# GpSimd makes the relative dst rows of a double tile ahead of its edge-list gathers, not behind them

## The reference, cut to what matters

```python
def reference(x, src, dst, edge_attr_64, W1, b1, W2, b2):      # x 6250x64, edge_attr 206250x64, dst sorted
    h = jnp.maximum(_layernorm(x, axis=-1), 0.0)
    msg = h[src] + edge_attr_64
    agg = jax.ops.segment_sum(msg, dst, num_segments=6250)
    return x + (jax.nn.relu(agg @ W1 + b1) @ W2 + b2)
```

## Time and profile before

| | |
|---|---|
| Time, median of 3 runs | 562.6 us (560.68 to 565.33) |
| Profiled execution | 561.41 us, its span 559.8 us |
| TensorE (PE) busy | 486.8 us, 87% of the span |
| VectorE (DVE) busy | 428.1 us, 76% |
| ScalarE (ACT) busy | 355.1 us, 63% |
| GpSimd (POOL) busy | 268.7 us, 48% |
| Mean DMA rate | 132 GB/s |

### The profile page before, as it was taken

One profiled execution on the slowest core, in us unless ns is written; L12 is line 12 of the kernel. 1 busy time (PEld: TensorE's weight loads), 2 busy tenths in 40 slices (PEclk: granted clock), 3 DMA queues, 4 the chain that ended last, 5 costly groups with the idle time before them and its releaser, 6 DMA issues.

```text
span 559.8 us, 27476 instructions
## 1 busy us (share of the span) xinstructions
PE 486.8 (87%) x12541; PEld 427.6 (76%) x12541; DVE 428.1 (76%) x456; ACT 355.1 (63%) x503; POOL 268.7 (48%) x249
## 2 busy tenths in 40 slices
PE   1014999999999999999999999999999999998996
PEld 1013788777888888888888888888888888887895
DVE  4999879667887797777787787777788779766941
ACT  3747667665766767656666666666676676575721
POOL 4483774484375366336357347417437535416200
PEclk9999999998999999989999999999999999899999
DMA  9575167453453543633634635435546354354300
GB/s 201 162 216 165 24 200 193 127 167 105 112 176 102 154 141 100 188 102 97 189 105 117 174 101 150 140 99 151 141 110 180 100 154 138 97 152 123 94 7 9
DMA packets 139623, 73.62 MB, mean 132 GB/s; under 512 B 23644, under 2 KB 137550, under 8 KB 139382
## 3 DMA queue, kind: packets, MB, share of 16 engines
q1 hardware_dynamic: 136105, 65.30, 42.4%
q0 software_dynamic: 3168, 4.90, 2.7%
q10 hardware_dynamic: 234, 1.65, 0.9%
HBM read 66.98 MB, written 4.86 MB: 128 GB/s over the span
## 4 chain that ended last, share of the span: by engine, by line
PE 84%; DVE 8%; issue 5%; ACT 1%; DMA 1%; another core or an unknown queue 0%; SPq 0%; DVEq 0%; ACTq 0%
PE sum_ps L823 25%; PE sum_ps L845 20%; PE count_ps L810 18%; PE sum_ps L831 14%; PE head_ps L860 3%; PE head_ps L867 3%; DVE lo_hot L656 2%; PE turn_ps L795 1%; DVE hi_hot L656 1%; DMA dst_sb<-in_dst 1%; DVE h_sb L555 1%; DVE mean L553 1%; DVE h_sb L568 1%; DVE var L561 1%; DVE h_parts L624 1%
## 5 line engine op out<-in xcount | busy, mean ns | idle before, releaser
L387 ACT CAST counts<-count_ps 128x784 bf16<-128x784 f32 x391 | 300.9, 817 | 129.0 <-PE count_ps L810 124.6
L656 DVE TENSOR_TENSOR lo_hot<-iota_lo,codes 128x4096 bf16<-128x4096 bf16 x98 | 224.1, 2286 | 66.8 <-PE count_ps L810 54.4
L823 PE MATMUL sum_ps<-counts,h_parts 128*128 128x256 bf16 (+1 forms) x1225 | 153.8, 277 | 0.0
L845 PE MATMUL sum_ps<-e_hot,edges 128*64 128x24 f32 x3528 | 129.6, 215 | 15.8 <-issue 15.6
L810 PE MATMUL count_ps<-hi_hot,lo_hot 64*128 64x49 bf16 x6256 | 124.9, 184 | 19.1 <-DVE hi_hot L656 11.5
L845 PEld LDWEIGHTS sum_ps<-e_hot,edges 128*64 128x64 f32 x3528 | 124.9, 138 | 20.5 <-issue 19.3
L810 PEld LDWEIGHTS count_ps<-hi_hot,lo_hot 64*128 64x128 bf16 x6256 | 101.5, 95 | 42.8 <-issue 13.4
L823 PEld LDWEIGHTS sum_ps<-counts,h_parts 128*128 128x128 bf16 x1225 | 114.1, 100 | 20.2 <-issue 0.2
L479 POOL TENSOR_SCALAR r_f<-rp_f 1x2 f32<-1x2 f32 x24 | 12.8, 533 | 188.9 <-DVE rp_f L630 188.8
L469 POOL DMA_INDIRECT g<-in_dst,row_i x49 | 88.0, 1796 | 18.3 <-issue 11.5
L656 DVE TENSOR_TENSOR hi_hot<-iota_hi,codes 128x1600 bf16<-128x1600 bf16 x98 | 96.5, 985 | 0.0
(11 more groups left out here) (108 smaller groups left out, 222.3 us busy)
## 6 DMA issues: line engine op xcount, KB each, us to landing
edges<-in_edge_attr SPq DMA_DIRECT2D x98, 576.0 KB
h_rows<-h_sb SPq DMA_DIRECT2D x1, 1568.0 KB, 10.1
x_sb<-in_x SPq DMA_DIRECT2D x4, 384.0 KB, 10.5
out<-o_sb SPq DMA_DIRECT2D x24, 64.0 KB, 3.7
comb_rows<-counts ACTq DMA_DIRECT2D x1, 1443.8 KB
dst_rows<-in_dst SPq DMA_DIRECT2D x49, 18.0 KB
ell<-comb_rows,ell_idx POOLq DMA_INDIRECT x50
g<-in_dst,row_i POOLq DMA_INDIRECT x49
```

Of the source, the lines that this page charges most:

```text
L387: nc.scalar.copy(counts[j % 2][:, :, 0:2 * half].rearrange("p s (h i) -> p h s i", h=2)[:, :, :, 8 * u:8 * u + 8], count_ps[g % 2][:, :, 0 ...
L656: return nc.vector.tensor_tensor(out_ap.rearrange("p i (a t) -> p i a t", t=2), bc(table_ap.rearrange("p (o a t) -> p o a t", o=1, t=2), [ ...
L823: nc.tensor.matmul(sum_ps[m % 2][:, 0:cols], parts[:, s, 0:2 * F], counts[m % 2][:, s, 0:cols], start=(s == 0), stop=False, skip_group_che ...
L845: last = nc.tensor.matmul(sum_ps[m % 2][half, low:low + W], edges[t % SLOT_EDGES][:, c, k * F:(k + 1) * F], e_hot[h][:, i, :], start=False ...
```

## The change

`make_rel(j - 1)` moves ahead of `gather_slots(j)` in GpSimd's loop. Nothing is added or taken away, and the waits of both stay as they are.

```diff
                     place_ranges(j)
                     if j == 0:
                         pool.wait_ge(comb_out, 48)
-                    gather_slots(j)
                     if j >= 1:
                         make_rel(j - 1)
+                    gather_slots(j)
                     if j >= 2:
                         add_bias(j - 2)
                 add_bias(DTS - 2)
```

## The result

The change made the kernel **faster on the chip where both were first compared**: 545.38 us median of four runs (543.06 to 555.27) against 562.28, a ratio of 0.968 (95% interval 0.963 to 0.973). I had forecast 566 us, so the sign was wrong. Later, on another chip, the kernel before took 531.85 us and the same changed kernel 561.94 to 583.01. Times are medians of all runs, while a ratio compares only those runs of each kernel that lie within about 1.5% of its fastest.

What follows compares the result with a forecast made beforehand. The prediction took TensorE, 84% of the chain, as the bound, so only its waits cost time. Early +1.2, +1.6 and +0.3, late 0 and tail +1.0 summed to +4.1 us, forecast 566 us (+0.7%), range 561 to 573.

Steps and rivals of the forecast that it cites:

- Late stretch: Turns 6 to 23: VectorE's pause covers the moved operation and lists land before they are wanted; 0 us.
- Early stretch: Turns 1 to 5: list gathers end 1.55 us later; terms +1.2 (turn 2), +1.6 (turn 3), +0.3 us (turns 4 and 5).
- Tail: Last turns: last list gathers end some 1.9 us later and TensorE has no slack; +1.0 us.
- Sum: Whole kernel: 1.2 + 1.6 + 0.3 + 0 + 1.0 = +4.1 us, bounds 1.7 and 8.1 us.
- Rival 1: Turns 3 to 5 and tail: later lists still land when the loads ahead land; about +1.5 us, 564 us; chance 0.20.
- Rival 2: Turn 1: moved operation misses the gap before `lo_hot`, shutting GpSimd out; +5.2 us, about 571 us in all; chance 0.11.
- Rival 3: Later turns: closed loop of lists, tables, pointers and gathers stays slow; 597 us, or about 575 if partly; chance 0.08.
- Rival 4: Turn 1: GpSimd's moved operation holds VectorE, `lo_hot` starts 0.97 us later; +1.0 us, 567 us; chance 0.07.
- Rival 5: Early turns: faster by the 0.3 us and an operation no longer disturbing `e_hot`; about 561 us; chance 0.04.

Runs made afterwards that it cites:

- e4: The change in GpSimd's turns 6 to 23 only, all other turns in the order of the kernel before: 535.83 us, ratio 0.956 to the kernel before.
- 532 kind: The four groups of runs in which the kernel before took 531.7 to 533.9 us (29 runs, highest 546.16).
- e11: The change in GpSimd's turns 1 to 5 only, against the kernel before on the 532 kind: 540.34 us, ratio 1.015.
- e13: The changed kernel run again on a chip of the 532 kind: 561.94, 578.03, 577.32 and 583.01 us, against 531.85 for the kernel before.
- 561 kind: The four groups of runs in which the kernel before took 560.6 to 562.3 us (43 runs, lowest 549.01).
- e14: The kernel before, unchanged, run for its trace on a chip of the 532 kind: eight runs of it there between 530.36 and 546.16 us, median 531.85.
- e12: The change in turns 4 to 23 only, against the kernel before on the 532 kind: four runs of 577.0, 573.21, 530.44 and 530.96 us.
- e16: Kernel before, second list gather left out every other turn from 6, six gathers in a row added in turn 24: 560.08 us, against 561.47.
- e15: The change in turns 6 to 23 only, with six indirect DMAs in a row added in turn 24, on the 532 kind: 564.0 us.
- e5: Kernel before with only 2 of 18 chunks of edges loaded from tile 12 on: 558.97 us, against 560.93.

## Why the prediction was wrong, point by point

- **Late stretch, "Term: 0": this step failed.** What it says of GpSimd's own way holds: VectorE's pause, the moved operation of 1.16 us, the second gather under the tables, no wait for lists. What failed is the premise that TensorE is then the bound, so that a turn of 20.1 us was all TensorE's own work. 1.4 us of it were TensorE's lateness beside GpSimd's gathers, in some 18 turns: e4 measures -24.8 us for this term. The profile had it: "issue" was 5% of the chain, and I went past it. Also, I had the first gather ahead of `lo_hot`; without the lateness `lo_hot` comes 1.2 us sooner and holds it, 2.33 us.
- **Early stretch: right in kind, too small.** Its unit holds: from the end of `r_i` to the end of the second gather took 4.85 us before and 6.45 after in turn 2 on the 532 kind, 1.60 more against my 1.55. But the sum starts with turn 2, and of turn 1 it has only the 0.3 us taken off. In that turn the second gather ran at 37.22 for 3.86 us, under VectorE's long subtraction, and ended 4.3 us later than before. `match`, which had no wait at 43.52, came at 46.52:
```profile
46.52 0.48 DVE L642 SCALAR_TENSOR_TENSOR hi_m<-ell,node_f 128x64 bf16<-128x64 f32 x2 [3.17 <-DMA ell<-comb_rows,ell_idx]
```
  TensorE waited 2.99 us for `hi_hot` at 50.16, and GpSimd's next `r_f` was 3.0 us later, at 57.30 against 54.31. The same first delay of 3.0 to 3.1 us is in the traces of e11 and e13. With all turns, e11 has +8 where I had 3.1. The premise that the moved waits find their events done failed too: one for `dst_rows` took 4.17 us in the profiled execution, until 105.64.
- **Tail, +1.0: right in kind, too small.** The last gathers ended 16.14 us behind TensorE's mark at 489.45, against 14.07 behind 499.44 before: 2.1 us later, where I had 1.9. The flight to `hi_m` was 2.90 us, the long one of my two, so nothing was hidden, and TensorE waited 2.51 us for `hi_hot`:
```profile
504.14 1.45 POOL L496 DMA_INDIRECT ell<-comb_rows,ell_idx  x1 [0.30 <-issue]
...
508.49 0.48 DVE L642 SCALAR_TENSOR_TENSOR hi_m<-ell,node_f 128x64 bf16<-128x64 f32 x2 [3.71 <-DMA ell<-comb_rows,ell_idx]
...
512.33 0.58 PE L810 MATMUL count_ps<-hi_hot,lo_hot 64*128 64x49 bf16 x32 [2.51 <-DVE hi_hot L656]
```
  Behind this wait the granted clock fell (0.57 in 513 to 517 us), so the tail cost more than the wait: from the mark at 489.45 to the last one took 42.6 us, against 39.1 before from 499.44, +3.5 us.
- **Sum.** On the 561 kind e4, which leaves the last turn as it was, has -24.8; with +2.5 to +3.5 of the tail, the -16.9 measured leaves +4.4 to +5.4 for the early part, by comparison over two chips.
- **Rival 1** (the flight takes it back) did not happen: the waits for lists grew, 31.4 us against 13.3. Its own sum is off by a little: 1.2 + 0.5 and a little is 1.7 or more, not 1.5.
- **Rival 2** (the first moved operation misses its gap) did not happen: it ran at 33.40 for 1.15 us. Yet 3.0 us of its price of 5.2 came, by the second gather of that turn, as said above.
- **Rival 3** (the slow loop stays), to which I gave 0.08, is what happens on the 532 kind, at 562 to 583 us where I had put 575 and 597. I looked for what frees the loop in the fall of the clock at 127 us. In e14 it is left in a turn in which GpSimd finds VectorE pausing: `r_f` took 0.22 us at 153.46, where it had taken 2.12; there, too, the clock was at 0.50 shortly before, from 149.4 to 152.8 us. Why one execution finds that turn and the next doesn't (e12) stays open.
- **Rival 4** (VectorE held): `lo_hot` started at 33.69, inside the moved operation of 33.40 to 34.55. The Trainium skill, page "SBUF — State Buffer", section "Who interferes with whom", has a `tensor_tensor` with both inputs in SBUF contend with GpSimd's reads; taken as the exclusive lock of that section, it would have held `lo_hot` until 34.55. This trace does not agree.
- **Rival 5** (faster) had the right sign with 0.04 on it, but by another cause and down to 561 us only.

## What to carry to other kernels

Time of the bounding engine that is put down to "issue" need not be its own work: divide a turn into runs of like instructions, and where the same 36 matmuls take 2.5 us here and 1.1 elsewhere, look at what another engine does beside them. Whether an engine is late or only drawn so is told by those that wait for its results. Where engines feed each other in a closed loop, a delay of a few us is not paid once but can decide when the loop is left, so price the first turn too, read several executions, and put a change in only behind the turn where the loop is left. A ratio from one chip can have the other sign on the next: compare on more than one.

## What the runs showed of the hardware

- Beside an indirect DMA of GpSimd (0.94 to 1.06 us), TensorE's matmuls started in bunches of about 5 with holes of 0.4 to 0.5 us, and VectorE and ScalarE got its results late, in four of eight groups of runs, and next to never in the others. Six in a row (7.3 us) made a turn 8.2 us longer (e16 against e15), a part of it by the clock. What links the two inside the chip is open. Edge loads at full size are not needed (e5), VectorE's tables neither (e16).
- A gather stretched by VectorE's tables did TensorE no harm, though it fetched the same lists: with 2.33 and 1.50 us for the two, the 36 edge matmuls took 1.12 us in place of 2.52.
- A gather that began under VectorE's `lo_hot` ended with `hi_hot`: from 305.28 to 307.61, where `hi_hot` ended at 307.61.
- Beside the six gathers of e16 the granted clock fell: 1.00 in 518 to 523 us, 0.51 in 523 to 544, so that the 36 edge matmuls at 529.96 took 2.07 us against 1.18.
